# Edge network of a graph kernel: one tile in sixteen built from node rows on chip instead of gathered

## The reference

```python
h = jnp.maximum(_layernorm(x, axis=-1), 0.0)
edge = jnp.concatenate([x[source], x[target], edge_feat], axis=-1)   # here x is h
h = jax.nn.relu(edge @ W1 + b1)          # W1: (48 + 48 + 16) x 128
h = jax.nn.relu(h @ W2 + b2)             # W2: 128 x 128
message = h @ W3 + b3                    # W3: 128 x 48
msum = jax.ops.segment_sum(message, target, num_segments=n)
update = msum / jnp.maximum(cnt, 1.0)[:, None]
return x + update
```

## Time and profile before

| | us |
|---|---|
| median of 3 runs | 6174.53 |
| lowest and highest | 6171.81 to 6194.94 |
| span of the profiled execution, first to last instruction | 6161.4 |
| what lies around the span, against the median | 13.1 |

### The profile page before, as it was taken

One profiled execution on the slowest core, in us unless ns is written; L12 is line 12 of the kernel. 1 busy time (PEld: TensorE's weight loads), 2 busy tenths in 40 slices (PEclk: granted clock), 3 DMA queues, 4 the chain that ended last, 5 costly groups with the idle time before them and its releaser, 6 DMA issues. The chain is left out here.

```text
span 6161.4 us, 148527 instructions
## 1 busy us (share of the span) xinstructions
PE 5105.3 (83%) x40298; PEld 4259.0 (69%) x40299; DVE 3550.1 (58%) x11415; ACT 1709.0 (28%) x3091; POOL 4073.1 (66%) x3903
## 2 busy tenths in 40 slices
PE   4885999999999768778888877787787888888877
PEld 4883899999999656666666666666666666666666
DVE  8998999999996643443434434434344343434444
ACT  3336666666663321111111111111111111111110
POOL 0106667666664467777777777777777777777776
PEclk9998999999999888888888888888988888888888
DMA  9206999999999733333333333333333333333332
GB/s 165 32 0 161 278 289 288 288 291 290 290 291 271 177 107 83 83 85 83 85 83 83 85 84 83 85 83 84 84 83 85 83 84 84 84 84 84 83 85 66
DMA packets 653787, 816.43 MB, mean 133 GB/s; under 512 B 426282, under 2 KB 471052, under 8 KB 653114
## 3 DMA queue, kind: packets, MB, share of 16 engines
q1 hardware_dynamic: 478251, 592.65, 32.8%
q0 software_dynamic: 175360, 221.63, 17.0%
HBM read 563.36 MB, written 250.47 MB: 132 GB/s over the span
## 5 line engine op out<-in xcount | busy, mean ns | idle before, releaser
L1729 POOL DMA_INDIRECT p_got<-p_tab,idx_d x3128 | 2962.5, 947 | 964.4 <-issue 864.2
L1715 ACT ACTIVATE h<-z,b_col 128x512 f32<-128x512 f32 x782 | 537.6, 687 | 3391.9 <-PE z L1855 3343.6
L1719 DVE TENSOR_TENSOR h<-z,nb 128x512 f32<-128x512 f32 x782 | 540.9, 692 | 1606.3 <-PE z L1695 1598.6
L1689 PEld LDWEIGHTS z<-ident_f,p_got 128*128 128x128 f32 x3128 | 415.8, 161 | 1385.5 <-DMA p_got<-p_tab,idx_d 1239.8
L1689 PE MATMUL z<-ident_f,p_got 128*128 128x128 f32 x3128 | 596.9, 323 | 784.9 <-DMA p_got<-p_tab,idx_d 784.7
L1073 PE MATMUL a_ps<-tile_r,pair_l 128*128 128x288 fp8e5 x5280 | 1041.4, 287 | 75.4 <-DVE tile_r L1160 45.5
L910 POOL DMA_INDIRECT sum_tab<-val_s,idx_s x496 | 788.9, 1590 | 466.9 <-ACT val_s L1027 332.5
L1094 PE MATMUL out_ps<-gw,a_got 121*128 121x144 bf16 x11340 | 1076.4, 225 | 4.5 <-DMA a_got<-a_tab 4.2
L1695 PEld LDWEIGHTS z<-w_sb,h 128*128 128x128 f32 x6256 | 1033.5, 234 | 56.4
L1695 PE MATMUL z<-w_sb,h 128*128 128x128 f32 x6256 | 1023.6, 318 | 0.0
L1036 ACT CAST stage<-a_ps 128x576 uint16<-128x576 f32 x1320 | 838.6, 640 | 405.0 <-PE a_ps L1073 397.4
(11 more groups left out here) (202 smaller groups left out, 3692.9 us busy)
## 6 DMA issues: line engine op xcount, KB each, us to landing
a_tab<-stage SPq DMA_DIRECT2D x330, 576.0 KB
a_got<-a_tab SPq DMA_DIRECT2D x330, 576.0 KB
rel<-rel_row SPq DMA_DIRECT2D x391, 192.0 KB
p_got<-p_tab,idx_d POOLq DMA_INDIRECT x3128
ef<-in_edge_t SPq DMA_DIRECT2D x391, 64.0 KB
q_win<-q_tab SPq DMA_DIRECT2D x782, 24.0 KB
src_bc<-src_row SPq DMA_DIRECT2D x124, 128.0 KB
a_tab<-big SPq DMA_DIRECT2D x22, 472.5 KB
```

The source lines that it names most:

```text
L1689: pe.matmul(out_tile, p_rows[:, j, :], ident_f[:, :], start=False, stop=False, is_transpose=True, skip_group_check=True)
L1729: pool.indirect_dma_start(p_rows[:, j, :], None, p_tab, bass.IndirectOffsetOnAxis(idx[:, j:j + 1], 0)).then_inc(landed, 16)
```

## The change

In two of the eight groups of a loop body (places 0 and 4) the last tile of the four is no longer gathered. Its 128 columns of 48 values are copied one by one out of `h_all`, the transposed node rows of all nodes, which now stay on chip in `big`. VectorE copies half of the columns and ScalarE the other half. TensorE multiplies the tile of columns (`h_col`) by the source part of W1 (`w1a_sb`) in the place of the transpose of gathered rows. The first eight groups are gathered whole.

The columns of a tile are made in four quarters, one in each of four steps of the loop, so that in every step each of the two engines copies 16 columns in two lots of 8. For a lot, one call reads 8 source indices (16 bits each) from `own_idx` into 8 registers, without a check of their bounds, and each copy takes its address from one of them. SyncE loads the 128 indices of a tile with one more DMA from a new table `own_row`; the table is written early, by the same transposes that make `src_row`.

To keep `h_all`, ScalarE in the node stage copies each block of `h_t` once more. The sums by node move out of `big` to a buffer of their own; they are cleared half by VectorE and half by ScalarE at the start of the edge network, no longer by GpSimd at the end of the node stage. The counts move to partition 64 of `big`. In the last stage some semaphores are shared; its operations are the same.

```diff
+OWN = (0,4)
+OWN_TILE = GROUP - 1
+QUARTERS = 4
+LOT = 8
...
+    OWN_STEP = DEPTH // len(OWN)
+    OWNS = NG // OWN_STEP
...
-        seg_acc = big[:, 0:NPP]
+        h_all = big[0:F, 0:NPP]
+        CNT_AT = 2 * SPAN
+        cnt_acc = big[CNT_AT:CNT_AT + 1, 0:NPP]
...
+                        wait_past(act, h_t_ready, 2 * (k - 2))
                         act.copy(h_t[0:F, :, :], t_ps_c[:, 0:CB, :]).then_inc(h_t_ready, 1)
+                        act.wait_ge(h_t_ready, 2 * (k - 2) + 1)
+                        act.copy(h_all[:, (k - 2) * CB * P:(k - 1) * CB * P],
+                                 h_t[0:F, :, :].rearrange("p c n -> p (c n)")).then_inc(h_t_ready, 1)
...
-                pool.wait_ge(agg_ready, NK)
-                pool.memset(seg_acc, 0.0).then_inc(t_zero, 1)
-                pool.wait_ge(t_zero, 4)
...
-        def src_part(pe, z1, p_rows):
-
-            for j, out_tile in enumerate(each_tile(z1)):
-                pe.matmul(out_tile, p_rows[:, j, :], ident_f[:, :], start=False, stop=False, is_transpose=True,
+        def src_part(pe, z1, p_rows, tiles=range(GROUP)):
+
+            for j in tiles:
+                pe.matmul(each_tile(z1)[j], p_rows[:, j, :], ident_f[:, :], start=False, stop=False, is_transpose=True,
...
+        def gather(pool, p_rows, idx, landed, tiles=range(GROUP)):
+            for j in tiles:
                 pool.indirect_dma_start(p_rows[:, j, :], None, p_tab, bass.IndirectOffsetOnAxis(idx[:, j:j + 1], 0)
                                         ).then_inc(landed, 16)
 
...
+        seg_acc = sb("seg_acc", [P, NPP], F32)
...
+            w1a_sb = sb("w1a_sb", [P, H], F32, life)
+            h_col = [sb(f"h_col{b}", [P, P], F32, life) for b in range(len(OWN))]
+            own_idx = [sb(f"own_idx{b}", [1, P], U16, life) for b in range(len(OWN))]
...
+                def owned(q, s):
+                    return s in OWN and past(q, DEPTH)
+
+                def gathered_tiles(q, s):
+                    return [j for j in range(GROUP) if j != OWN_TILE or not owned(q, s)]
+
...
+                def building(q, s):
+
+                    for b, slot in enumerate(OWN):
+                        k = (s - slot - 1) % DEPTH
+                        after = DEPTH - 1 - k
+                        if k < QUARTERS and (not isinstance(q, int) or DEPTH <= q + after < NE):
+                            yield b, slot, k, after
+
+                def columns(eng, engine, copy, b, first, copied):
+
+                    for lot in range(2):
+                        at = first + lot * LOT
+                        _, nodes = nc.values_load_multi_w_load_instructions(
+                            own_idx[b][0:1, at:at + LOT], engines=[engine], min_val=0, max_val=N - 1,
+                            skip_runtime_bounds_check_because="they are the sources of edges, each below N")
+                        for i, node in enumerate(nodes):
+                            last = copy(h_col[b][0:F, at + i:at + i + 1], h_all[:, bass.ds(node, 1)])
+                        last.then_inc(copied[b], 1)
 
                 def half_of(pair, s):
...
+                            sp.dma_start(w1a_sb[0:F, :], w1ab[:, 0:H]).then_inc(w_loaded, 16)
+                        for b, slot in enumerate(OWN):
+                            if s == (slot + QUARTERS) % DEPTH and (not isinstance(q, int) or DEPTH <= q + QUARTERS < NE):
+                                sp.wait_ge(cols_made[b], (q + (QUARTERS - slot)) * 2)
+                                sp.sem_inc(sp_turns, 1)
+                                group = sp.snap(nc.s_assert_within((q + QUARTERS) // OWN_STEP, 0, OWNS - 1)) if not isinstance(q, int) \
+                                    else (q + QUARTERS) // OWN_STEP
+                                sp.dma_start(own_idx[b][:, :], own_row[bass.ds(group, 1), :]).then_inc(own_loaded[b], 16)
...
+                        for b, slot, k, after in building(q, s):
+                            if k == 0:
+                                act.wait_ge(own_loaded[b], (q + (after - slot)) * 2)
+                                act.sem_inc(any_turn, 1)
+                            columns(act, mybir.EngineType.Activation, act.copy, b, (2 * k + 1) * 2 * LOT, cols_made)
...
+                    act.copy(seg_acc[:, SEG_CUT:], zero_b[:, 0:1].to_broadcast([P, NPP - SEG_CUT])).then_inc(cnt_zero, 1)
...
+                        pe.wait_ge(gathered[s % UNROLL], rows_landed(q, s))
+                        src_part(pe, z1[k], p_got[s % UNROLL], gathered_tiles(q, s))
+                        if owned(q, s):
+                            b = OWN.index(s)
+                            pe.wait_ge(cols_made[b], (q + (COLS - s)) * 2)
+                            pe.sem_inc(pe_turns, 1)
+                            pe.matmul(each_tile(z1[k])[OWN_TILE], w1a_sb[:, :], h_col[b][:, :], start=False, stop=False,
...
+                    dve.memset(seg_acc[:, 0:SEG_CUT], 0.0).then_inc(cnt_zero, 1)
...
+                        for b, slot, k, after in building(q, s):
+                            if k == 0:
+                                dve.wait_ge(own_loaded[b], (q + (after - slot)) * 2)
+                                dve.sem_inc(any_turn, 1)
+                                wait_past(dve, z1_made, q)
+                                dve.sem_inc(any_turn, 1)
+                            columns(dve, mybir.EngineType.DVE, dve.tensor_copy, b, 2 * k * 2 * LOT, cols_made)
```

More of the change, by code:

```diff
@@ L201, in build_gnn @@
     src_row = dram("src_row", [SG, W], U16)
+    OWN_STEP = DEPTH // len(OWN)
+    OWNS = NG // OWN_STEP
+    assert OWN == tuple(range(0, DEPTH, OWN_STEP)) and OWN_STEP >= QUARTERS and P == QUARTERS * 4 * LOT
+    assert max(g for g in range(NE) if g % DEPTH in OWN) * GROUP + OWN_TILE < EDGES // P
+    own_row = dram("own_row", [OWNS, P], U16)
     g_tab = dram("g_tab", [NPP, PLANES * F], BF16)
@@ L636, in _ @@
                 for c in range(SG * GROUP // TURNED):
-                    last = pe.transpose(turned_ps[:, c, :], src_s[:, c * TURNED:(c + 1) * TURNED], ident_f[:, :])
+                    pe.transpose(turned_ps[:, c, :], src_s[:, c * TURNED:(c + 1) * TURNED], ident_f[:, :])
+                for c in range(OWNS // OWN_ROWS):
+                    last = pe.transpose(own_ps[:, c, :], own_f[:, c * OWN_ROWS:(c + 1) * OWN_ROWS], ident_f[:, :])
                 last.then_inc(turned, 1)
@@ L1703, in sum_by_node @@
             for j in range(GROUP):
-                last = pe.matmul(seg_ps[0:1, nodes:2 * nodes], ones_b[:, :], hot_c[:, j, :], start=(j == 0),
-                                 stop=(j == GROUP - 1))
+                last = pe.matmul(seg_ps[:, nodes:2 * nodes], ones_b[:, :].to_broadcast([P, P]), hot_c[:, j, :],
+                                 start=(j == 0), stop=(j == GROUP - 1))
             return last
@@ L1769, in build_gnn @@
                 gathered = [sem(f"gathered{s}", ctx) for s in range(UNROLL)]
+                own_loaded = [sem(f"own_loaded{b}", ctx) for b in range(len(OWN))]
+                cols_made = [sem(f"cols_made{b}", ctx) for b in range(len(OWN))]
                 cnt_turned = sem("cnt_turned", ctx)
@@ L1785, in slot_count, with rows_landed @@
                     return in_slot(q, s, DEPTH, per)
+                COLS = P // LOT // 2
+                SEG_CUT = NPP // 2
+                def owned(q, s):
+                    return s in OWN and past(q, DEPTH)
+                def gathered_tiles(q, s):
+                    return [j for j in range(GROUP) if j != OWN_TILE or not owned(q, s)]
+                def rows_landed(q, s):
+                    own = [slot in OWN for slot in range(s % UNROLL, DEPTH, UNROLL)]
+                    cycle = GROUP * len(own) - sum(own)
+                    before = s // UNROLL
+                    if isinstance(q, int) and q < DEPTH:
+                        return (before + 1) * GROUP * 16
+                    return (q - s) // DEPTH * (cycle * 16) + (GROUP * (before + 1) - sum(own[:before + 1]) + sum(own)) * 16                         if isinstance(q, int) else (q - s) * (cycle * 16 // DEPTH) + (
+                            GROUP * (before + 1) - sum(own[:before + 1]) + sum(own)) * 16
+                def building(q, s):
[13 more added lines that the diff above has]
+                        last.then_inc(copied[b], 1)
                 def half_of(pair, s):
@@ L1826, in step @@
                         pool.sem_inc(pool_turns, 1)
-                        gather(pool, p_got[s % UNROLL], half_of(idx[s // 2], s), gathered[s % UNROLL])
+                        gather(pool, p_got[s % UNROLL], half_of(idx[s // 2], s), gathered[s % UNROLL], gathered_tiles(q, s))
                     paced(pool, NE, step, DEPTH)
@@ L1837, in step @@
                         make_h1(act, h1[s % 2], z1[s % 2]).then_inc(h1_ready, 1)
+                        for b, slot, k, after in building(q, s):
[4 more added lines that the diff above has]
```

(9 more changed lines are left out.)

73 lines of the change are left out of this document (41 added, 32 removed).

## The result

The changed kernel takes 8607.18 us (median of 4 runs, 8605.25 to 8615.7) against 6184.06 us for the kernel before on the same chip: a ratio of 1.3923, 95% interval 1.3892 to 1.3955. The forecast was 6004 us, and the range ended at 7010.

The account below looks back on a forecast made before the run. POOL's gathers were taken as the clock, 5.01 us a group. 6161.4 (span) + 13.1 (around it) - 178 (groups at 4.78 us) + 7 (node stage) gave 6004 us; the 8-in-10 range was 5930 to 7010.

Parts of the forecast that it names:

- its largest unknown: Edge network, VectorE: how eight indices in one read are priced, from 0.69 to 4.40 us for both reads of a group.
- the lower end: VectorE's index reads: one read costs the same whatever it brings, 0.305 + 0.04 us, 0.69 us for both.
- The first rival: VectorE's index reads: each further value in a read has its own price, giving 6360 to 8800 us; chance 0.28.
- 4.68 + 14p: VectorE's time for a group in us, with p us for each further value read; slower than before from p = 0.024.
- The third rival: Edge network loop: the longer body is fetched again each turn, 2.0 to 3.1 us a wait, 6197 us; chance 0.08.
- The estimate of the body: VectorE's loop body grows by some 270 instructions: 128 copies, as many register steps and 16 reads.
- The value of the removed gathers: Edge network, POOL: 194 gathers fewer at 1.252 us each, 243 us at most, leaving 4.70 us a group.
- A column at 0.125 us: VectorE's single-column copies with a register step each: 16 a group take 2.00 us, between 1.3 and 3.0.
- VectorE's own 1.99 us: VectorE's existing work in an edge network group, 1.99 us, with the first node's register read costed at nothing.
- the second rival: VectorE's 0.82 us ahead of L1913, waiting for sums and reading a register, stays exposed: 5.50 us a group, 6561 us; chance 0.10.
- The node stage and the clearing of the sums: Second block copies add 7 us, between 0 and 14; clearing on VectorE and ScalarE adds nothing, or 5 us if not.
- ScalarE with room to spare: ScalarE's work, copies and reads take 3.3 us a group in the edge network, hidden under 4.70 with 1.4 to spare.

Follow-up runs that it names:

- the kernel with one value a read: Against the changed kernel, each lot reads one index; its eight columns are copied singly from that node and the seven behind it: 6357 us, ratio 1.0305.
- one wide copy: Against the changed kernel, each lot reads one index and makes a single copy 8 columns wide from there: 5926 us, 0.9615 of the kernel before.
- the run of the side parts: Changed kernel with all tiles gathered, without copies, index reads and SyncE's extra DMA; second block copy, moved sums, counts and index table stay: 6173 us, 1.0003.
- the pairs: Changed kernel with one tile in 32 ungathered, not two, and eight 16-bit indices read as four 32-bit values, then split: 6047 us, ratio 0.9803.
- the two reads of four: Against the changed kernel, each lot of eight indices is read as two reads of four 16-bit values: 8728 us, ratio 1.4156.

## Why the prediction was wrong

The step that failed is the one that the prediction called its largest unknown: "I take the lower end as the likeliest, since the read is one instruction on each engine and the eight values lie in 16 neighbouring bytes". One instruction it is, and the values are neighbours, but each 16-bit value has its own price of 0.22 us: 1.827 us for a read where 0.305, and 0.04 for a gap, were taken. Two of them add 3.65 us to a group of VectorE in place of 0.69, and VectorE's sequencer, no longer POOL, sets the pace. The first rival had the right mechanism and nearly the right formula: 4.68 + 14p with p = (1.827 - 0.305) / 7 = 0.217 gives 7.72 us a group, and 7.61 was measured. I gave it a chance of 0.28 and ended the range at p = 0.1, where nothing in the rows spoke for an end. The Trainium skill's figure of about 200 ns a register (Runtime: NRT & Kernel Launch, section on instruction fetch mechanics) is given there for reads from HBM; it came close for this kernel's 16-bit reads from on-chip memory, 0.22 us a value, and does not hold for 32-bit ones, where four came in 0.343 us.

The third rival came true as well, on top of the first and not in its place. I priced it at 2.0 to 3.1 us a turn; it is 2.5 us behind the branch and 0.7 inside the copies, 3.2 us a turn. In the measured kernel that is 774 / 8 x 3.2 = 310 us of the loss. It would have spoiled the forecast by itself, for it is more than the 178 us of gain that was forecast: the kernel with one value a read has plain groups of 4.70 us, as the sum had them, and is 3.05% slower than before. The estimate of the body was good (some 270 instructions more; 411 against 134 were counted). The prediction gave this 0.08 and treated the rivals as exclusive. The rule of the Trainium skill, in the section named above, that a taken branch to a block no longer held waits for a DMA agrees with the 2.7 to 3.0 us behind the branch and with the packets. The remaining 1.2 us a turn, 774 / 8 x 1.2 = 116 us, stood in no term of the sum; part of it is 0.2 to 0.3 us in each of the two groups where a tile's first quarter begins.

The rest, by its steps:

- The value of the removed gathers, 243 us and 4.70 us a group: right, 244 us and 37.53 us a turn with one wide copy.
- A column at 0.125 us: 0.115 measured, 1.84 us for 16.
- VectorE's own 1.99 us, with the read of the first node hidden: right to within 0.2 us. From L1982 to L2008's start, 4107.14 to 4109.16, are 2.02 us, and no idle stretch stands ahead of L2006, so the second rival (0.82 us exposed) is out.
- The node stage and the clearing of the sums: 3 us where 7 were taken, in the run of the side parts. That run has neither the matmul nor SyncE's extra DMA; that these cost nothing is shown by the kernel of one wide copy, which has both and turns in the time of 30 gathers.
- TensorE's clock was no term of the sum. The granted clock of the 500 us behind 4000 us is 0.61, a mean between its two levels of 1.2 and 2.4 GHz, where it was 0.89 before; TensorE does 1418 matmuls there in place of 2297 and waits for `hot_t` in each group. That the clock follows from these waits is argued: no run changes it alone.
- ScalarE with room to spare: wrong by the same reads. It needs 0.7 + 16 x 0.093 + 2 x 1.715 = 5.6 us, more than the 5.01 of before; VectorE's 7.61 hides it.

The turn as measured, with nothing else, gives 6174.5 + 774 x (65.33 / 8 - 5.01) = 8618 us, against 8607, so no cost of this size is left outside the edge network.

## What to carry to other kernels

Price a register read by its values and their width before building on it: here eight 16-bit values took 1.83 us, eight 32-bit values 0.60. When an engine with slack is given many small instructions, count the instructions of its loop body too: on VectorE, counted in the traces from branch to branch, bodies of 187, 267 and 273 instructions stayed in, bodies of 305, 411 and 427 were fetched anew in each turn. A count alone does not decide it, as the next section shows. Two unlikely costs on one engine add up; a range must hold their sum.

## What the hardware showed that was not expected

- A sequencer's read of 16-bit values costs 0.22 us a value on VectorE (one 0.287, four 0.947, eight 1.827); of 32-bit values four cost 0.343 and eight 0.597. ScalarE: 0.263, 0.884 and 1.715; 0.308 and 0.547.
- With loop bodies of 305 instructions or more on VectorE, its sequencer stood still for 2.7 to 3.3 us behind the branch in each turn, and for 0.2 us or less with 273 or fewer. The code packets come five a turn for each engine that stands still. In the kernels with ten a turn (changed, one value a read, eight 32-bit values) ScalarE stands still behind its branch too, 2.3 to 3.4 us; in those with five (the pairs, the two reads of four) it goes on at once, as here in the kernel with two reads of four:

```profile
L71 ACTq COMPARE_BRANCH  x1: 53/53/53, 4059.5 to 4059.5; - x1
L71 ACTq FUSED_REGOPS  x1: 50/50/50, 4059.8 to 4059.8; - x1
```

  ScalarE's body has 300 instructions in the first and 316 in this last one. So the longer body stayed in and the shorter did not, and the number of instructions is not all that counts. What else does, where the code begins for one, no run here tests.
- Two chips ran the same kernel before at 6170 and 7106 us. In kernels traced on both, single instructions have the same length (a gather 0.944 and 0.947 us), with stops in between on the slower chip that are not explained.
